# Patch embedding that starts with strip 1 in full rows, an early function table, and strip differences on GpSimd

## The reference, cut to what matters

```python
shifts = ((1, -1, 1, -1), (-1, 1, -1, 1), (-1, 1, 1, -1), (1, -1, -1, 1))
parts = [x] + [_shift2d(x, HALF * s[2], HALF * s[0]) for s in shifts]   # 5 images, shifted by half a patch
xc = jnp.concatenate(parts, axis=1)
...                                       # patches of 16 x 16: [128, 16 tokens, 3840]
mu = patches.mean(axis=-1, keepdims=True)
var = patches.var(axis=-1, keepdims=True)
xn = (patches - mu) * jax.lax.rsqrt(var + LN_EPS) * ln_gamma + ln_beta
return jnp.einsum('bnp,dp->bnd', xn, W) + b          # DIM = 192
```

## Time and profile before

| | |
|---|---|
| median of 3 runs | 598.61 us (598.5 to 599.84) |
| profiled execution: span, first to last instruction | 604.2 us (the page gives no other time of it) |
| TensorE busy | 495.1 us, 82% |
| VectorE busy | 319.2 us, 53% |
| ScalarE busy | 206.6 us, 34% |
| GpSimd busy | 154.5 us, 26% |
| mean granted TensorE clock | 0.909 |

### The profile page before, as it was taken

One profiled execution on the slowest core, in us unless ns is written; L12 is line 12 of the kernel. 1 busy time (PEld: TensorE's weight loads), 2 busy tenths in 40 slices (PEclk: granted clock), 3 DMA queues, 4 the chain that ended last, 5 costly groups with the idle time before them and its releaser, 6 DMA issues.

```text
span 604.2 us, 12487 instructions
## 1 busy us (share of the span) xinstructions
PE 495.1 (82%) x4400; PEld 457.5 (76%) x4401; DVE 319.2 (53%) x1037; ACT 206.6 (34%) x441; POOL 154.5 (26%) x148
## 2 busy tenths in 40 slices
PE   4999999986443596799998399767999999999960
PEld 4999996575442485799997286756999999999950
DVE  1668999788999786122221356892222222222207
ACT  3630014868984164233334052260121112121110
POOL 1592000000001002465433000005444543443220
PEclk9999999999567686999999589879999999999995
DMA  8995000000009123587779900022666655667117
GB/s 314 408 335 160 15 1 1 1 3 1 0 2 312 30 105 118 168 210 192 162 234 322 295 4 0 1 106 59 190 190 192 201 164 164 190 182 211 34 49 291
DMA packets 40659, 84.86 MB, mean 140 GB/s; under 512 B 7270, under 2 KB 23186, under 8 KB 39586
## 3 DMA queue, kind: packets, MB, share of 16 engines
q1 hardware_dynamic: 33218, 72.81, 37.0%
q0 software_dynamic: 7392, 11.41, 8.3%
HBM read 70.33 MB, written 13.86 MB: 139 GB/s over the span
## 4 chain that ended last, share of the span: by engine, by line
PE 69%; DVE 16%; DMA 6%; ACT 4%; issue 2%; another core or an unknown queue 1%; POOL 0%; SPq 0%; DVEq 0%; ACTq 0%; POOLq 0%
PE ps L1137 18%; PE ps L887 14%; PE ps L1113 12%; PE ps L1121 6%; DMA made<-xT,to_i 3%; DVE h L1924 2%; PE ps L827 2%; PE ps L1002 1%; PE ps L974 1%; DVE xT L1771 1%; PE ps L975 1%; PE ps L1104 1%; PE ps L867 1%; PE ps L868 1%; PE ps L852 1%
## 5 line engine op out<-in xcount | busy, mean ns | idle before, releaser
L1137 PE MATMUL ps<-arena,xn 128*128 x696 | 123.1, 327 | 2.1 <-ACT xn L777 2.1
L1137 PEld LDWEIGHTS ps<-arena,xn 128*128 128x128 f32 x696 | 111.8, 190 | 4.2 <-issue 4.0
L515 POOL DMA_INDIRECT xT<-rows,from_i x58 | 56.3, 971 | 175.8 <-DVE from_i L1785 127.5
L530 POOL DMA_INDIRECT made<-xT,to_i x58 | 67.8, 1170 | 100.9 <-DVE xT L1823 65.9
L887 PE MATMUL ps<-arena 128*128 128x192 f32 (+1 forms) x588 | 85.6, 336 | 9.0 <-ACT arena L556 9.0
L887 PEld LDWEIGHTS ps<-arena 128*128 128x128 f32 (+1 forms) x588 | 83.9, 196 | 9.3 <-ACT arena L556 8.6
L1113 PE MATMUL ps<-xn,arena 128*128 128x128 f32 x696 | 87.2, 275 | 3.2 <-DVE xn L1813 3.2
L1113 PEld LDWEIGHTS ps<-xn,arena 128*128 128x128 f32 x696 | 84.9, 192 | 3.5 <-issue 3.5
L780 ACT ACTIVATE xn<-ps 128x384 f32<-128x384 f32 x78 | 32.6, 493 | 144.7 <-PE ps L1123 110.0
L1811 DVE COPY xn<-ps 128x128 f32<-128x128 f32 x58 | 16.9, 292 | 118.9 <-PE ps L1105 98.2
L777 ACT ACTIVATE xn<-ps,b_all 128x128 f32<-128x128 f32 x114 | 30.8, 389 | 63.5 <-PE ps L1123 51.9
(11 more groups left out here) (373 smaller groups left out, 765.6 us busy)
## 6 DMA issues: line engine op xcount, KB each, us to landing
arena<-ffn_a SPq DMA_DIRECT2D x58, 384.0 KB
arena<-ffn_b SPq DMA_DIRECT2D x116, 96.0 KB
arena<-x_blocks SPq DMA_DIRECT2D x16, 384.0 KB, 7.0
arena<-x_strips SPq DMA_DIRECT2D x3, 1536.0 KB, 12.2
arena<-ffn SPq DMA_DIRECT2D x4, 1152.0 KB
rows<-xn SPq DMA_DIRECT2D x8, 384.0 KB, 2.3
arena<-made SPq DMA_DIRECT2D x8, 384.0 KB, 6.6
arena<-tok_w SPq DMA_DIRECT2D x8, 288.0 KB, 7.3
```

What stands on the lines that cost most here:

```text
L515: pool.indirect_dma_start(sx[:, k % 6], None, F["src"], bass.IndirectOffsetOnAxis(from_i[:, k:k + 1], 0)).then_inc(sem(f"sx_in{k % 6}"), 16)
L530: pool.indirect_dma_start(F["made"], bass.IndirectOffsetOnAxis(to_i[:, k:k + 1], 0), yo[:, k % 3], None, compute_op=(ALU.add, ALU.bypass)[ ...
L1137: mm = pe.matmul(ps[:, result_bank(k, N), 0:DIM], hT[:, u % 2, 128 * c:128 * c + 128], F["w2"][:, bass.ds(e2 + DIM * c, DIM)], start=(c == ...
```

## The change: what it does

TensorE starts with strip 1 and the lower half weights in full rows, and does strip 0 in row tiles after it. SyncE loads, in this order, the lower half weights (P = 1) by column with strip 1's two column halves, and then the upper half weights with strip 0's. `TRIPLES` goes by half and then by column. ScalarE asks for the table of its copy function ahead of its first wait. The differences of strips move from VectorE to GpSimd, behind the weight sums. `w_row` moves behind the first four groups of block statistics, GpSimd's sums no longer wait for it, and the bias rows are made one column later. Several semaphores are merged into shared counts.

```diff
-TRIPLES = [(P, b) for b in COLS for P in range(2)]
+TRIPLES = [(P, b) for P in (1, 0) for b in COLS]
...
-            weights_in(-1)
-            sp.dma_start(xs[:, 0, 1::2], x_strips[:, 0, 1::2]).then_inc(sem("x0_in1"), 16)
-            weights_in(1)
-            sp.dma_start(xs[:, 0, 0::2], x_strips[:, 0, 0::2]).then_inc(sem("x0_in0"), 16)
-            weights_in(0)
-            weights_in(2)
-            sp.dma_start(xs[:, 1], x_strips[:, 1]).then_inc(sem("x_in1"), 16)
+            for P, strip in ((1, 1), (0, 0)):
+                weights_in(P, -1)
+                columns_in(strip, 1)
+                weights_in(P, 1)
+                columns_in(strip, 0)
+                weights_in(P, 0)
+                weights_in(P, 2)
...
-            pool.wait_ge(sem("w_row"), 1)
+            pool.wait_ge(sem("wg_scaled"), len(TRIPLES))
+            pool.wait_ge(sem("wg_added"), 4)
...
+            def less(n, strip):
+                pool.wait_ge(sem(("strip_read", "tok_ps")[n]), n + 1)
+                pool.wait_ge(sem("x_in2"), 16)
+                for odd in (1, 0):
+                    pool.tensor_tensor(xs[:, strip, odd::2], xs[:, strip, odd::2], xs[:, 2, odd::2],
+                                       ALU.subtract).then_inc(sem("x_less"), 1)
+            less(0, 1)
+            less(1, 3)
...
+            act.preload_act_table(ACT.Copy)
...
             for n, b in enumerate(COLS):
+                weights_there(1, n)
+                for c, j in columns(b):
+                    mm = part("y0", j, 1, slice(0, 128), w_of(1, b, c), b, c)
+            mm.then_inc(sem("strip_read"), 1)
+            for n, b in enumerate(COLS):
+                weights_there(0, n)
+                for c, j in columns(b):
+                    mm = part("y0", j, 0, slice(64, 128), w_of(0, b, c), b, c)
                     part("y3", j, 0, slice(0, 64), w_of(1, b, c), b, c)
+            mm.then_inc(sem("tok_ps"), 1)
...
-                    if (name, b) == ("m2", 1):
+                    if (name, b) == ("m2", 0):
-                        pe.wait_ge(sem("cst_in"), 16)
+                        pe.wait_ge(sem("cst_in"), 32)
...
-            dve.tensor_tensor(w_row, wg[:, 0:12, :], wg[:, 12:24, :], ALU.add).then_inc(sem("w_row"), 1)
             for m in range(16):
...
+                if m == 3:
+                    dve.wait_ge(sem("wg_added"), 4)
+                    dve.wait_ge(sem("wg_scaled"), len(TRIPLES))
+                    dve.tensor_tensor(w_row, wg[:, 0:12, :], wg[:, 12:24, :], ALU.add).then_inc(sem("w_row"), 1)
...
-            less(0, 1)
             token_row(0)
-            less(1, 3)
             token_row(1)
```

More of the change, by code:

```diff
@@ L354, in _, with weights_in, columns_in @@
         def _(sp):
[L355 to L360, removed]
+            def weights_in(P, b):
+                if P and inner(b):
+                    sp.dma_start(w_un[:, 3 * b:3 * b + 3, :], tok_w_un[:, 3 * b:3 * b + 3, :]).then_inc(sem(f"w_in{P}{b}"), 16)
+                k = w_chunk(P, b)
+                sp.dma_start(w_sh[:, k:k + 3, :], tok_w[:, k:k + 3, :]).then_inc(sem(f"w_in{P}{b}"), 16)
+            def columns_in(strip, odd):
+                sp.dma_start(xs[:, strip, odd::2], x_strips[:, strip, odd::2]).then_inc(sem(f"x{strip}_in{odd}"), 16)
             def blocks_in(start, end):
@@ L378, in _ @@
             sp.dma_start(cst[:], consts).then_inc(sem("cst_in"), 16)
-            sp.dma_start(tok_b_row[:], tok_b).then_inc(sem("tok_b_in"), 16)
+            sp.dma_start(tok_b_row[:], tok_b).then_inc(sem("cst_in"), 16)
             blocks_in(4, 8)
@@ L398, in _ @@
             sp.dma_start(gate_w1[1][0:K1], gate1_w[128:DIM, :]).then_inc(sem("gate_in"), 16)
-            sp.wait_ge(sem("cst_in"), 16)
+            sp.wait_ge(sem("cst_in"), 32)
             sp.dma_start(made0[TOKS:TOKS + 128 * TILES0, :].rearrange("(k p) c -> p k c", p=128),
@@ L440, in _ @@
             sp.dma_start(F0["w2"], ffn0_2).then_inc(sem("ffn_in0"), 16)
-            sp.dma_start(b2_all, ffn0_b2.to_broadcast([128, E0 * DIM])).then_inc(sem("b2_in"), 16)
+            sp.dma_start(b2_all, ffn0_b2.to_broadcast([128, E0 * DIM])).then_inc(sem("ffn_in0"), 16)
             sp.wait_ge(sem("o_ps"), 4)
@@ L505, in _ @@
                 pool.tensor_tensor(s[:, 0, :], s[:, 0, :], s[:, 2, :], ALU.add).then_inc(sem("w_sums"), 1)
+            def less(n, strip):
[6 more added lines that the diff above has]
+            less(1, 3)
             pool.wait_ge(sem("o_ps"), 4)
-            pool.memset(aqT1[K1:K1 + 3], 1.0).then_inc(sem("ones_row"), 1)
+            pool.memset(aqT1[K1:K1 + 3], 1.0).then_inc(sem("pool_set"), 1)
             def exchange(F):
@@ L553, in _ @@
                 k = w_chunk(P, b)
-                act.wait_ge(sem(f"w_in{b}"), 48 if inner(b) else 32)
+                act.wait_ge(sem(f"w_in{P}{b}"), 32 if P and inner(b) else 16)
                 for c in range(k, k + 3):
@@ L810, in _ @@
             ins.then_inc(sem("lin_a"), 1)
-            act.wait_ge(sem("gate_logit"), 1)
-            act.activation(stat[:, 501:502], stat[:, 500:501], ACT.Exp, scale=-1.0).then_inc(sem("gate_exp"), 1)
+            act.wait_ge(sem("exp_in"), 1)
+            act.activation(stat[:, 501:502], stat[:, 500:501], ACT.Exp, scale=-1.0).then_inc(sem("exp_out"), 1)
             transposed(3)
-            act.wait_ge(sem("soft_in"), 1)
+            act.wait_ge(sem("exp_in"), 2)
             d16 = rt[:, 432:448]
-            act.activation(d16, d16, ACT.Exp).then_inc(sem("soft_exp"), 1)
+            act.activation(d16, d16, ACT.Exp).then_inc(sem("exp_out"), 1)
             all_norms(1)
@@ L860, in logits @@
                 if i == 0:
-                    pe.wait_ge(sem("gate_set"), 2)
+                    pe.wait_ge(sem("pool_set"), 3)
                 pe.wait_ge(sem("xT0_ready"), 4 * (1 + 2 * n) + i + 1)
@@ L915, in turned_weights @@
                 return mm
-            for n, (name, strip, P) in enumerate((("y0", 1, 1), ("y3", 3, 0), ("m2", 2, 2), ("y1", 1, 0), ("y2", 3, 1))):
-                if n < 3:
+            for n, (name, strip, P) in enumerate((("y3", 3, 0), ("m2", 2, 2), ("y1", 1, 0), ("y2", 3, 1))):
+                if n < 2:
                     pe.wait_ge(sem(f"x_in{strip}"), 16)
@@ L954, in _ @@
             pe.wait_ge(sem("bias_in"), 16 * BIASES)
-            pe.wait_ge(sem("ones_row"), 1)
+            pe.wait_ge(sem("pool_set"), 1)
             def qk_free(n):
@@ L1062, in _ @@
             pe.wait_ge(sem("aq_act"), 5)
-            pe.wait_ge(sem("ones_row"), 2)
+            pe.wait_ge(sem("pool_set"), 5)
             pe.wait_ge(sem("wp_ready"), 2)
@@ L1338, in _ @@
                 ins.then_inc(sem("wg_added"), 1)
-            for n in range(4):
-                dve.wait_ge(sem("wg_added"), n + 1)
-            dve.wait_ge(sem("wg_scaled"), len(TRIPLES))
-            dve.tensor_tensor(w_row, wg[:, 0:12, :], wg[:, 12:24, :], ALU.add).then_inc(sem("w_row"), 1)
             for m in range(16):
@@ L1443, in token_row @@
                 layer_norm(TOK_ROWS[n], count)
[L1445 to L1451, removed]
             above, group = rt[:, 0:9], rt[:, 16:24]
@@ L1460, in _ @@
             affine(3)
-            less(0, 1)
             token_row(0)
-            less(1, 3)
             token_row(1)
-            dve.wait_ge(sem("wnat_set"), 1)
+            dve.wait_ge(sem("pool_set"), 4)
             dve.wait_ge(sem("wnat_in"), 128)
@@ L1498, in _ @@
             dve.tensor_tensor(gate_b[:], gate_b[:], gate_c[:], ALU.subtract)
-            dve.wait_ge(sem("cst_in"), 16)
+            dve.wait_ge(sem("cst_in"), 32)
             dve.tensor_copy(iota_bf[:], cst[:, C_IOTA128:C_IOTA128 + 128])
@@ L1736, in route @@
                     link(dve.tensor_tensor(d16, c16, a16, ALU.subtract))
-                    dve.tensor_tensor(d16, d16, stat[:, 464:480], ALU.mult).then_inc(sem("soft_in"), 1)
+                    dve.tensor_tensor(d16, d16, stat[:, 464:480], ALU.mult).then_inc(sem("exp_in"), 1)
                 dve.wait_ge(sem("rank_ps"), n + 1)
@@ L1799, in route @@
                 if n:
-                    dve.wait_ge(sem("soft_exp"), 1)
+                    dve.wait_ge(sem("exp_out"), 2)
                     link(dve.tensor_scalar(c16, d16, 1.0, None, ALU.add))
@@ L1832, in copies @@
                 if n == 0:
-                    dve.wait_ge(sem("b2_in"), 16)
+                    dve.wait_ge(sem("ffn_in0"), 32)
                 dve.wait_ge(sem(f"tiles_ready{n}"), 1)
@@ L1893, in _ @@
             link(dve.tensor_tensor(ltmp[:, 0:16], ps[:, 6, 0:16], cst[:, C_SEL:C_SEL + 16], ALU.mult))
-            dve.tensor_reduce(stat[:, 500:501], ltmp[:, 0:16], AX.X, ALU.add).then_inc(sem("gate_logit"), 1)
+            dve.tensor_reduce(stat[:, 500:501], ltmp[:, 0:16], AX.X, ALU.add).then_inc(sem("exp_in"), 1)
             plus_normed(12, 16)
-            dve.wait_ge(sem("gate_exp"), 1)
+            dve.wait_ge(sem("exp_out"), 1)
             link(dve.tensor_scalar(stat[:, 502:503], stat[:, 501:502], 1.0, None, ALU.add))
```

34 lines of the change are left out of this document (17 added, 17 removed).

## The result

| | before | after |
|---|---|---|
| median of 4 runs each | 599.23 us (598.5 to 599.9) | 607.84 us (603.92 to 610.19) |
| ratio, 95% interval | 1 | 1.0141 [1.0102, 1.0179] |
| profiled execution: span | 604.2 us | 608.4 us (its own time 610.19: 1.8 us lie around the span) |
| first matmul | 8.98 us | 6.67 us |
| first copy of turned attention weights (last step ahead of the scores) | 98.30 us | 106.15 us |

The forecast was 596.8 us, faster. The start came as forecast and a little better, and more than four times of it was lost before 107 us. The delay of 7.85 us at the first copy is still 8.36 us at the first gather; the medians differ by 8.6.

A forecast was written before the change was run, and what follows sets the result against it. TensorE's own chain from its first matmul (8.98 us) to 97.66 us was taken as the bound: 1.88 from the start, plus 0.17, less 0.25, gave 1.8 us, so 598.61 became 596.8 us; 8-in-10 range 595.2 to 598.9.

The forecast's parts named there:

- Differences on GpSimd: Strip differences moved off VectorE: 3.75 us each on GpSimd, four done from 48.7 to 63.7 us, in time for TensorE.
- C: Rival: GpSimd's differences late for TensorE's last two passes, slower than before from 2.62 times 3.75 us; 601.3 to 604.3; chance 0.07.
- VectorE's gain is no gain of time: VectorE loses two pairs of subtractions, 3.43 us each, but TensorE already gets its results in time: no gain.
- the 0.6 us stay: Margin at the scaled attention weights: ScalarE's scalings follow copies released by TensorE, so they move with it and 0.6 us remain.
- The 6.9 us that cover the later bias rows: VectorE's wait for bias sums ends 2.1 us later; the 6.9 us no longer spent on differences cover it.
- the way of the start: First matmul at about 7.1 us in place of 8.98, released by the landing of strip 1's half; gain 1.88 us.
- the next weights: Weights for columns 1 and 0 ready at 10.5 and 14.6 us: no wait left, 0.17 us gained.
- the row tiles: Row-tiled part now in the middle, two changes of form instead of one: cost 0.25 us, bounds 0 and 0.5.
- the low clock: TensorE's first microseconds run at 1.2 GHz, a loss of 2.2 us, taken as the same before and after.
- A: Rival: the clock takes the start's gain back, or the strip lands no earlier; 0.9 us gain, 597.7; chance 0.24.
- B: Rival: TensorE's low-clock stretch is shorter with full rows from the first matmul; 3.3 us gain, 595.3; chance 0.15.
- the early table: ScalarE's table load ahead of its first wait: worth nothing by itself, since 7.0 us without it is under 7.1.

The follow-up runs named there:

- less_on_vector: Changed kernel with the strip differences back on VectorE at their old places: 603.87 us against 598.32 for the kernel before, ratio 1.0071.
- bias_early: Changed kernel, differences on VectorE, bias rows one column earlier, attention-weight transposes behind the last column: 601.8 us against 600.53 for the kernel before, ratio 0.9976.
- less_in_blocks: bias_early with strip 1's difference inside VectorE's block statistics and bias rows as in the changed kernel: 598.32 us against 600.53 before, ratio 0.998.
- blocks_filled: less_in_blocks plus 18 dummy TensorE transposes ahead of its wait at the attention weights' transposes: 600.53 us against 599.98 for the kernel before, ratio 1.003.
- no_preload: bias_early without ScalarE's early table load: 601.08 us in one run, against 600.53 for the kernel before.

## Why the prediction was wrong

**The step that failed is "Differences on GpSimd".** It asked only whether GpSimd would be in time for TensorE, and there it was right: 3.44 us each (3.75 by proportion), done at 64.8, wanted at 65.8 and later, and no wait of TensorE names GpSimd. It then took the neighbourhood of two-input work as a price on GpSimd alone: "By the page alone it would be a cost only on GpSimd." The line that it drew on names the contention and not which engine pays. It also named only `affine` as the neighbour, and not the token scales, whose list runs from 47.8 to 56.1 us before, just where the differences were put. The price fell on VectorE: 12.5 us on four instructions (3.05 + 3.22 + 3.12 + 3.12) and 1.3 us on three more beside the weight sums, which themselves ended late. With VectorE's own 0.4 us, its scales ended 14.2 us later (70.3 against 56.1). No rival had this mechanism: C had GpSimd as the late one, and its point of decision was never approached. The bound above VectorE's cost should have been one whole GpSimd instruction for each VectorE instruction that could stand beside it. With the prediction's own 3.75 us, four of them are 15.0 us; less the 6.9 saved and the 0.6 in reserve, that is an estimate of 7.5 us: a rival on the slower side, by the rows of before and that bound alone.

**"VectorE's gain is no gain of time", and "the 0.6 us stay", failed with it.** The scaling of attention weights was taken to follow TensorE's copies. A row of VectorE's in the timeline of before, which I had not weighed, says otherwise:
```profile
91.01 0.17 DVE L1416 TENSOR_SCALAR stat<-stat 128x5 f32<-128x5 f32 x1
```
This last statistic for the weights ends at 91.18, and ScalarE begins at 91.22. ScalarE's copies, which TensorE's transposes release, end at 91.10: the two conditions were level to within 0.1 us, and only one of them moves with TensorE. The 0.6 us are VectorE's reserve against TensorE, and its list is a second chain nearly as long as the one on record. That TensorE's neighbours join end to end does not say that the others have room. Hence TensorE waits 3.2 us in less_on_vector, where no difference holds anything, and bias_early and less_in_blocks hand the start's gain to VectorE's sums.

**The 6.9 us that cover the later bias rows**: the two terms were sized well (`affine` 2.4 us later without holds; 2.1 forecast), the cover was not there, since the holds took twice of it.

**Right:** the way of the start, sized low (6.67, where 7.1 was taken and 6.8 was the lower bound: the strip's half landed 4.8 us after its issue at 1.68, so the shorter queue was worth about 1.6 us and not 1.0), no waits at the next weights, 0.23 us twice for the row tiles, swap of order free, the low clock about as costly as before (2.5 us against 2.2; A and B fell). **Wrong in a small way:** the early table, called worth nothing, is worth 0.1 to 0.45 us of start, because the strip landed before 7.0. And `w_row` "in idle time" held GpSimd for 2.3 us, so that the weight sums ended at 51.1 and not 48.7, beside VectorE's scales.

**Open:** which of VectorE's instruction kinds are held was seen only for those in these rows. The later bias rows were not tried alone. No version ran faster than the kernel before: bias_early, less_in_blocks and blocks_filled equal it, and to turn the earlier start into time VectorE's list up to 97 us would have to be shortened by 2 us, which wasn't tried. About 1.4 us of these in bias_early are the holds by the late weight sums.

## What to carry to other kernels

Before work moves to GpSimd, list what VectorE does in the same microseconds: here two-input work on both, and VectorE's TENSOR_SCALAR too, was serial, a short VectorE instruction cost a whole GpSimd one, and neither splitting nor shifting the GpSimd work helped while VectorE was at work of that kind. Look for the second-longest chain before an early stage is made faster: its reserve (0.6 us here) bounds what the change can bring, and no version reached the scores more than 0.5 us earlier. A held engine counts as busy; compare one instruction's duration in two traces.

## What the runs showed of the hardware that was not expected

- GpSimd and VectorE take turns by whole instructions: 0.27 us became 3.32 beside 1536 elements, 0.18 became 0.92 beside 384; GpSimd's 1.41 us became 3.72 beside `w_row`. A reduction with one input was not held (0.22 us), and neither were VectorE's statistics (in before four of them on 192 elements take 1.14 us at 42.65, beside the weight sums, and at 65.13, with GpSimd idle).
- TensorE's wait of 2.07 us in less_in_blocks, with one of 1.38 us behind it, was followed by the lower level: the granted clock reads 0.50 from 101 to 103 us, and the fifth projection begins at 104.81, with the first wait filled at 103.10, so 1.7 us were lost. In no_preload, with 0.56 us and the same 1.38, it stays at 1.00. The wait of 7.5 us in after cost 2.2 us in this way.
